# A third-kernel stage with its landmark work reordered, its scaling moved to ScalarE, and idle products added on TensorE

## What is computed

```python
Q_l = Q.reshape(b, H, M, n // M, HD).mean(axis=-2)
K_l = K.reshape(b, H, M, n // M, HD).mean(axis=-2)
kernel2 = jax.nn.softmax(jnp.einsum('bhmd,bhkd->bhmk', Q_l, K_l), axis=-1)
kernel3 = jax.nn.softmax(jnp.einsum('bhmd,bhnd->bhmn', Q_l, K), axis=-1)
SV = jnp.matmul(jnp.matmul(kernel1, iterative_inv(kernel2)), jnp.matmul(kernel3, V))
# iterative_inv starts from: V = swapaxes(K, -1, -2) / max(sum(K, axis=-2))
```

## Time and profile before

| | us |
|---|---|
| median of 3 runs | 2015.58 |
| lowest, highest | 2012.86, 2019.72 |
| the profiled execution | 2023.81 |
| its span, first to last instruction | 2022.1 |
| the stage of the change in it | 1305.2 to 1463.2 |

### The profile page before, as it was taken

One profiled execution on the slowest core, in us unless ns is written; L12 is line 12 of the kernel. 1 busy time (PEld: TensorE's weight loads), 2 busy tenths in 40 slices (PEclk: granted clock), 3 DMA queues, 4 the chain that ended last, 5 costly groups with the idle time before them and its releaser, 6 DMA issues. The chain is left out here.

```text
span 2022.1 us, 34369 instructions
## 1 busy us (share of the span) xinstructions
PE 1766.0 (87%) x11923; PEld 939.2 (46%) x12009; DVE 1534.9 (76%) x3643; ACT 1008.7 (50%) x1909; POOL 542.0 (27%) x625
## 2 busy tenths in 40 slices
PE   0898946899999999999999959978867888999998
PEld 0565621223332323232323236655565656888854
DVE  7997659898988989898999938558666994444466
ACT  3454422566767676767676826345512553222210
POOL 0343243000000000000150010136504884666610
PEclk9998976999999999999999979968787999999999
DMA  3456575004040505050640164112225223566566
GB/s 104 151 198 221 184 193 114 2 2 162 2 161 2 161 2 162 2 161 2 179 150 12 43 212 168 56 46 90 73 77 199 93 93 122 188 190 186 169 226 219
DMA packets 162940, 241.33 MB, mean 119 GB/s; under 512 B 21939, under 2 KB 131507, under 8 KB 161107
## 3 DMA queue, kind: packets, MB, share of 16 engines
q1 hardware_dynamic: 126930, 155.08, 25.7%
q0 software_dynamic: 23136, 75.65, 10.6%
q10 hardware_dynamic: 12704, 8.39, 1.3%
HBM read 118.86 MB, written 119.82 MB: 118 GB/s over the span
## 5 line engine op out<-in xcount | busy, mean ns | idle before, releaser
L1118 ACT ACTIVATE c_prob<-c_pst 128x512 f32<-128x512 f32 (+1 forms) x1152 | 578.4, 578 | 299.4 <-PE c_pst L1083 123.4
L1226 DVE TENSOR_REDUCE c_mx<-c_pf 128x2 f32<-128x1024 f32 x384 | 459.5, 1221 | 32.8 <-PE c_pf L1060 29.3
L1079 PE MATMUL c_pst<-c_qa,c_ka 128*128 128x512 bf16 (+3 forms) x1194 | 339.2, 355 | 14.6 <-DMA c_qa<-c_mT 5.9
L1095 PE MATMUL c_po<-c_prob,c_vh 128*32 128x512 f32 (+3 forms) x2560 | 294.1, 541 | 0.8 <-ACT c_prob L1118 0.4
L1060 PE MATMUL c_pf<-c_ka,c_qa 64*128 64x512 bf16 (+3 forms) x1280 | 230.1, 366 | 49.5 <-DMA c_ka<-s_kbias 22.3
L1222 DVE CUSTOM_DVE_ANT_0 c_spare<-c_pf,c_cut 128x384 f32<-128x384 f32 (+3 forms) x512 | 230.8, 491 | 28.8 <-PE c_pf L1060 24.2
L1079 PEld LDWEIGHTS c_pst<-c_qa,c_ka 128*128 128x128 bf16 x1280 | 110.4, 97 | 203.9 <-ACT c_prob L1118 112.1
L1060 PEld LDWEIGHTS c_pf<-c_ka,c_qa 64*128 64x128 bf16 x1280 | 59.4, 93 | 309.5 <-DVE c_mx L1226 120.5
L992 POOL IOTA c_zero<- 128x24 int32 x6 | 1.3, 214 | 631.9 <-PE c_po L1095 631.9
L2209 POOL DMA_INDIRECT s_parts<-x_yr,x_tags x144 | 140.4, 975 | 86.2 <-DVE x_yr L2858 62.8
L2843 DVE TENSOR_TENSOR x_h<-x_ps,x_sg 128x256 f32<-128x256 f32 x72 | 30.5, 424 | 142.3 <-ACT x_sg L2812 134.8
(11 more groups left out here) (438 smaller groups left out, 3071.2 us busy)
## 6 DMA issues: line engine op xcount, KB each, us to landing
s_slots<-c_zero POOLq DMA_DIRECT2D x6, 3264.0 KB
x_xr<-s_slots SPq DMA_DIRECT2D x72, 272.0 KB
x_rows<-s_parts SPq DMA_DIRECT2D x8, 2048.0 KB, 8.9
c_qa<-s_qs SPq DMA_DIRECT2D x64, 192.0 KB, 7.7
c_ka<-s_ks SPq DMA_DIRECT2D x64, 192.0 KB, 8.7
s_qs<-b_parts SPq DMA_DIRECT2D x32, 256.0 KB, 2.4
s_ks<-b_parts SPq DMA_DIRECT2D x32, 256.0 KB, 2.6
s_vs<-b_va SPq DMA_DIRECT2D x32, 256.0 KB, 3.8
```

The source lines that it names most:

```text
L1079: mm = nc.tensor.matmul(pst[:, u % NS, at:at + qn], ka[:, s, hh, kt * P:(kt + 1) * P], qa[:, s, hh, qb * QB + q0:qb * QB + q0 + qn], start ...
L1095: mm = nc.tensor.matmul(po[HV * h:HV * h + HV, q0:q0 + qn], vh[:, s, kt, h, :], prob[:, a % NP, h, at:at + qn], start=(kt == 0), stop=(a i ...
L1118: nc.scalar.activation(prob[:, g % NP, hh, 0:w], pst[:, u % NS, 0:w], ACT.Exp).then_inc(exp_ok, 1)
L1226: nc.vector.tensor_reduce(mx[:, fh:fh + 2, qt, part], pf[:, slot, :, 0:kn], AX.X, ALU.max).then_inc(max_ok, 1)
```

## The change

Four edits, all in landmarks_and_kernel3. In the lists of PE and DVE the landmark entries move behind scores and maximum. POOL's marks_done goes; ACT's scale_marks takes its place, with four activations (copy, scaled by a column of cm) at the end of each of eight steps, from the one whose last entry has n = 5. PE gets idle_products: twelve bf16 products of constants, 128 x 128 by 128 x 256, into an unused part of the PSUM tile pw before all else, and six at the end of every step from n = 3 on, behind a wait for o_ok of pair n - 2. And the two 128 x 1 joins on DVE, of the maxima and of the row sums, become tensor_reduce.

```diff
@@ gpsimd
-            def marks_done():
-                pool.wait_ge(cm_ok, 1)
-                pool.wait_ge(bd_ok, 2)
-                nc.gpsimd.tensor_tensor(VTb[:], e2[:], over(cm[:], M), ALU.mult)
-                pool.wait_ge(kt_ok, 4)
-                nc.gpsimd.tensor_tensor(Vb[:], KTb[:], over(cm[:], M), ALU.mult)
...
-                if n == 6:
-                    marks_done()
@@ tensor
+            def idle_products(count):
+                for _ in range(count):
+                    nc.tensor.matmul(pw[:, P:3 * P], consts["below"][:], route_of["picked"][0].rearrange("p t e -> p (t e)"), start=True, stop=True)
+
+            idle_products(12)
...
             def turn_rest(n, bm, r):
                 turn_half(n, 1, r)
+                if n >= 3:
+                    wait(pe, o_ok, n - 1)
+                    idle_products(6)
...
-            staggered(pe, NPR, DEPTH, [(2, mark_sums), (2, mark_turn), (2, counts), (1, scores), (1, mark_products), (4, gather), (2, turn), (3, values), (2, turn_rest)], 4)
+            staggered(pe, NPR, DEPTH, [(1, scores), (1, mark_products), (2, mark_sums), (2, mark_turn), (2, counts), (4, gather), (2, turn), (3, values), (2, turn_rest)], 4)
@@ scalar
+            def scale_marks(n, bm, r):
+
+                first = 2 * (n - SCALED)
+                if n == SCALED:
+                    act.wait_ge(cm_ok, 1)
+                    act.wait_ge(kt_ok, 4)
+                if 0 <= first < NPR:
+                    for a in (first, first + 1):
+                        nc.scalar.activation(VTb[:, a, :], e2[:, a, :], ACT.Copy, scale=cm[:, a:a + 1])
+                        nc.scalar.activation(Vb[:, a, :], KTb[:, a, :], ACT.Copy, scale=cm[:, a:a + 1])
...
+            staggered(act, NPR, DEPTH, [(2, take_marks), (2, take_turned), (1, exp), (1, exp_marks), (1, place_marks), (2, take_rest), (2, scale_marks)], 4)
@@ vector
-                nc.vector.tensor_tensor(nmx[:, s:s + 1], nmh[:, s, 0:1], nmh[:, s, 1:2], ALU.min).then_inc(mx_ok, 1)
+                nc.vector.tensor_reduce(nmx[:, s:s + 1], nmh[:, s], AX.X, ALU.min).then_inc(mx_ok, 1)
...
-                nc.vector.tensor_tensor(rs[:, s:s + 1], sums[:, r, 0:1], sums[:, r, 1:2], ALU.add).then_inc(rs_ok, 1)
+                nc.vector.tensor_reduce(rs[:, s:s + 1], sums[:, r], AX.X, ALU.add).then_inc(rs_ok, 1)
...
-            staggered(dve, NPR, DEPTH, [(2, take_counts), (2, normalise_marks), (1, maximum), (1, shift_marks), (4, divide), (3, take_values), (2, route)], 4)
+            staggered(dve, NPR, DEPTH, [(1, maximum), (1, shift_marks), (2, take_counts), (2, normalise_marks), (4, divide), (3, take_values), (2, route)], 4)
```

More of the change, by code:

```diff
@@ L1859, in landmarks_and_kernel3 @@
     COUNT = 11
+    SCALED = 5
     RG = 4
@@ L2097, in take_marks @@
                     nc.scalar.copy(KTb[M:P, part], turned_marks[M:P, :, M:P]).then_inc(kt_ok, 1)
-            staggered(act, NPR, DEPTH, [(2, take_marks), (2, take_turned), (1, exp), (1, exp_marks), (1, place_marks), (2, take_rest)], 4)
+            def scale_marks(n, bm, r):
[8 more added lines that the diff above has]
+            staggered(act, NPR, DEPTH, [(2, take_marks), (2, take_turned), (1, exp), (1, exp_marks), (1, place_marks), (2, take_rest), (2, scale_marks)], 4)
         @block.vector
```

## The result

The changed kernel takes 2006.6 us (median of 9 runs, 2003.31 to 2014.49), the kernel before on the same chip 2016.94 (9 runs, 2010.46 to 2022.0): a ratio of 0.9938, 95% interval 0.9918 to 0.9958. That is faster by some 10 us, 2.6 from the forecast of 2004 and inside its range.

A forecast was written before the change was run, and what follows sets the result against it. A ring of waits, closed by DVE at 2.4 GHz and PE at 1.2, with POOL's scatter chain beside it; the ring's end at 1447.4, later than POOL's 1443.8, gave 15.5 us less, 2008.3, and 2004 for the median, range 1990 to 2015.

The forecast's parts named there:

- The start: Landmarks behind the scores at the stage's start: POOL's fourth group comes 7 us earlier, between 3.5 and 15.
- near 1323: Sign of being right: with the first scores at 1307.5, the second exponential starts near 1323.
- The ring: Waits among DVE, ACT and PE: ten steps from sixth to sixteenth bias take 72.1 us, tail 12.5, end 1447.4.
- The end: Stage's end: the later of the ring, 1447.4, and POOL's last landing, 1443.8, decides; 15.5 us less.
- The step from the profile to the median: From 2008.3 us on the profile's base, half of the 8.2 by which the median was lower: 2004.
- The full clock: Rival: clock holds at 2.4 GHz from the first scores on; 27 us less, 1993 for the median; chance 0.15.
- The scaling: Landmark scaling leaves POOL for ACT: 3.93 us off the ring, 3.8 off POOL's chain; activations of 0.21 cost nothing.
- The idle products: PE's added products: delay scores by about 0.2 us, 1 in all; higher clock gives 4.8, between 0 and 7.2.
- the rival by which it falls as often as before: PE's clock falls as often despite the products; 2.7 us less, 2013, no change that can be told; chance 0.16.
- the rival by which denser work of DVE holds them up: POOL's indirect DMAs take 0.2 us more each, 13 groups 10.4 more; 2011 us; chance 0.06.
- 2030: Rival of a slower kernel: PE falls to 1.2 GHz more often, seven slow steps lose 14 us; chance 0.08.
- within 5 us: Sign of being right, at the stage's end: POOL's last landing and DVE's last write lie within 5 us.

The follow-up runs named there:

- e3: The kernel before with only the new order of PE's and DVE's lists; 2012.05 us against 2020.49, ratio 0.9959.
- e2: The kernel before with the idle products alone; 2017.65 us against 2019.49, ratio 0.9983.
- e6: The kernel before with the third kernel's block ended without POOL's closing instruction; 2014.12 us against 2019.49, ratio 0.9967.
- e4: The kernel before with only the scaling moved to ACT and the two tensor_reduce; 2017.32 us against 2020.49, ratio 0.9984.
- e5: The changed kernel with the third kernel's block ended without POOL's closing instruction; 2003.22 us, ratio 0.9914 to the kernel before.

## Why the prediction came out right, and where its sum was wrong

**The start** was mis-sized: I took 7 us, "nearer the lower end", of 3.5 to 15; it is 13.9. The second exponential, which I had 3.8 earlier, came 2.6 earlier by the stage's clock with the order alone (e3) and 8.7 earlier in the change, at 1317.24 where I had named "near 1323" as a sign: behind the twelve products the first scores ran at 2.4 GHz, in passes of 0.69 us instead of 1.08. And "the third exponential [...] comes 3.4 to 5 earlier" failed: it came 7.3 earlier with the order alone and 11.1 in the change. e3 shows the reason for the first part: with PE's long wait gone the slow stretch behind it did not come either, and this needed no idle products. I had given the recovery there to the products alone. The order brings 10.0 us to the fourth tag, the products 4.4, each alone.

**The ring** gained more than I said: ten steps of 70.2 us (1351.66 to 1421.86) where I had 72.1, and 10.1 of tail where I had 12.5. With the start this puts its end at 1431.9 instead of 1447.4. What the ten steps gained was not divided as I had it: with POOL's scaling they took 79.9 (before), 78.7 (e3), 77.9 (e2) and 72.4 (e6), with ACT's and nothing else changed 69.8 (e4). So moving the scaling, for which I had 3.93, seems to have brought more than the sixes; how much, single profiles that differ by 7 us for one ring can't tell.

**The end** is the step that failed in kind: "The later decides". I compared the ring with POOL's last landing and left out the close behind it, 5.3 us, though the row of before with its gap of 7.34 showed it. With the close POOL was level with the ring in the profile of before and 12.5 us behind it after. The fourth group began at 1341.29, 8 us earlier than I had it, its 13 groups took 96.0 us to the last scatter's end where 7.27 each make 94.5, and the close took nearly the whole of that back. A ring 15 us better than forecast and a close that was forgotten gave a time that came right by luck.

**The step from the profile to the median** was a guess: I took half of 8.2 us off the gain. The span fell by 17.4 and the median by 10.3; the 6.9 by which the profile of before lay above its median, of nine runs, went whole.

**The full clock**, a rival at 0.15, put the fourth group at 1341.3, which is where it came. But the clock did not hold: behind a wait of 2.50 us PE's column sums took 3.75 us as before, and from 1322.1 to 1325.1 the granted clock was 0.50. Its time of 1993 did not follow, because it too ended at POOL's landing.

**The scaling** cost ACT 0.36 us an activation, not my 0.21; as they overlap, the four of a step took 1.1 us and not 0.85. The Trainium skill ("ScalarE: Activation LUTs", the section on what ACT_TABLE_LOAD costs) makes 0.33 of it, an estimate from its figures; the trace is nearer to that. The idle time covered it, as the rows of the result show, and the stall of 3.9 us went.

**The idle products** delayed the scores by 0.3 us instead of 0.2 in seven of the twelve steps from the fourth bias on, on the edge of what I had called wrong. The gain of 4.8 less 1 that I gave them for the ten steps is 0 to 3 by the profiles with and without the sixes. The granted clock over these steps rose from 0.79 to 0.98, so the rival by which it falls as often as before did not come.

**POOL's groups** did not grow: its 64 scatters take 994 ns on average against 1011, so the rival by which denser work of DVE holds them up did not come, and 2030 is far off.

Of the signs I had named the clock, the activations and POOL's tags (12 steps of 7.54 on average, one of them 8.94 with a wait of 3.39 for a landing) came as said; the second exponential came 6 us ahead of the sign's time, and "within 5 us" failed, POOL's last scatter alone ended 5.3 behind DVE's last write.

## What to carry to other kernels

Before you price a ring, list every engine's last instruction ahead of the stage's end and the gap from it to the next block's first one; a chain that ends level with the one you shorten takes the gain, and a close behind an engine's last DMA belongs to its chain. A part that seems to gain little beside the others can be taken out again once the real bound is moved: here the six products of each step. And where a clock is low, look first for the wait in front of it: the order alone brought the fourth tag 10.0 us forward and the products alone 4.4, though the intervals of the two times, 8.4 and 1.8 us less, just overlap. Before you size a gain from one profile, see how far two profiles of one kernel differ; here the same ring ended 12.9 us apart.

## What the runs showed of the hardware

- Behind 64 indirect DMAs of POOL its block took 5.3 us to close after the last landing (gaps of 7.21 us in the change and 1.89 without the close in e5 and e6).
- PE's clock came back through the stage's own work, without idle products, in both before (0.83 from 1326.2 to 1329.2) and e3 (1.00 from 1322.4 on). In before it was 0.50 again within PE's wait of 7.35 us; in e3 it stayed, with a wait of 2.05 at that place; in the change it was 0.50 behind one of 2.50.
- Two products of POOL in a row held one operation of DVE, a bias of 128x1, for the length of both: 4.09 us instead of 0.16.
